# New orders and longer lags in a software-pipelined two-layer attention and expert kernel

## The reference

```python
x = x + L0_xattn(layernorm(x), ctx, ctx)   # 16 heads of 8; q, k, v with biases; softmax; output weights
x = x + L0_ffn(layernorm(x))               # 8 experts, the 2 best by gate; every expert is computed densely
x = x + L1_xattn(layernorm(x), ctx, ctx)   # as the first, without biases
x = x + L1_ffn(layernorm(x))               # recurrent cell over the 128 rows, 64 steps of one tile each
```

## Time and profile before

| | us |
|---|---|
| median of 3 runs | 853.44 |
| lowest, highest | 852.15, 854.73 |
| the profiled execution's own time | 852.91 |
| its span in the profile | 851.1 |
| TensorE busy, mean granted clock | 825.9, 0.994 of full |
| ScalarE busy | 793.9 |
| VectorE busy | 768.9 |
| GpSimd busy | 682.4 |

### The profile page before, as it was taken

One profiled execution on the slowest core, in us unless ns is written; L12 is line 12 of the kernel. 1 busy time (PEld: TensorE's weight loads), 2 busy tenths in 40 slices (PEclk: granted clock), 3 DMA queues, 4 the chain that ended last, 5 costly groups with the idle time before them and its releaser, 6 DMA issues. The chain is left out here.

```text
span 851.1 us, 41480 instructions
## 1 busy us (share of the span) xinstructions
PE 825.9 (97%) x15270; PEld 741.3 (87%) x15270; DVE 768.9 (90%) x2778; ACT 793.9 (93%) x2490; POOL 682.4 (80%) x1292
## 2 busy tenths in 40 slices
PE   6899999999999999999999999999999999999886
PEld 4688899999999999999999999999999999898674
DVE  6789999999999999999999999999999999989845
ACT  5899999999999999999999999999999999989764
POOL 5788988888888888888888888888888888878624
PEclk9999999999999999999999999999999999999999
DMA  9400000000000000000000000000000000000005
GB/s 330 183 3 3 2 3 4 3 3 4 3 3 3 3 4 3 4 3 3 3 3 3 3 3 3 4 3 3 4 3 3 4 3 4 3 3 3 3 3 198
DMA packets 6965, 17.67 MB, mean 21 GB/s; under 512 B 752, under 2 KB 2288, under 8 KB 6768
## 3 DMA queue, kind: packets, MB, share of 16 engines
q1 hardware_dynamic: 6480, 14.44, 4.5%
q10 hardware_dynamic: 288, 0.60, 0.2%
HBM read 10.84 MB, written 4.19 MB: 18 GB/s over the span
## 5 line engine op out<-in xcount | busy, mean ns | idle before, releaser
L824 DVE TENSOR_REDUCE mx<-ps 128x8 f32<-128x512 f32 (+1 forms) x288 | 173.1, 622 | 8.1 <-PE ps L321 7.7
L838 DVE TENSOR_TENSOR Ex<-ps,mx 128x512 f32<-128x512 f32 (+1 forms) x288 | 172.9, 621 | 0.2 <-issue 0.2
L1076 POOL TENSOR_TENSOR h<-Ex 128x512 f32<-128x512 f32 (+1 forms) x144 | 166.9, 1159 | 3.6 <-ACT Ex L632 3.3
L643 ACT ACTIVATE ET<-ps 128x512 f32<-128x512 f32 (+1 forms) x288 | 156.8, 546 | 6.9 <-PE ps L336 6.6
L632 ACT ACTIVATE Ex<-Ex 128x512 f32<-128x512 f32 (+1 forms) x288 | 162.7, 597 | 0.0
L336 PE MATMUL ps<-w,Ex 128*128 128x128 f32 x1024 | 162.3, 277 | 0.0
L681 ACT ACTIVATE hT<-ps,w 128x128 f32<-128x128 f32 x512 | 145.8, 374 | 11.2 <-PE ps L401 4.8
L930 DVE SCALAR_TENSOR_TENSOR acc<-ps,we,acc 128x128 f32<-128x128 f32 x448 | 148.4, 331 | 3.9 <-PE ps L422 1.3
L401 PEld LDWEIGHTS ps<-xT,w 128*128 128x128 f32 x1024 | 124.1, 191 | 24.6 <-issue 24.6
L401 PE MATMUL ps<-xT,w 128*128 128x128 f32 x1024 | 141.8, 281 | 0.0
L1060 POOL TENSOR_TENSOR rs<-ve,half 128x4 f32<-128x4 f32 (+3 forms) x77 | 71.6, 930 | 83.7 <-DVE ve L814 80.6
(11 more groups left out here) (108 smaller groups left out, 1785.7 us busy)
## 6 DMA issues: line engine op xcount, KB each, us to landing
cx<-ctx_dram SPq DMA_DIRECT2D x7, 512.0 KB, 12.9
x<-x_dram SPq DMA_DIRECT2D x7, 512.0 KB, 13.7
out_dram<-x SPq DMA_DIRECT2D x14, 256.0 KB, 2.7
w<-weights_dram SPq DMA_DIRECT2D x2, 512.0 KB, 6.4
w<-weights_dram SPq DMA_DIRECT2D x1, 576.0 KB, 8.7
out_dram<-x SPq DMA_DIRECT2D x4, 128.0 KB, 2.6
w<-weights_dram ACTq DMA_DIRECT2D x1, 328.0 KB, 4.1
w<-weights_dram ACTq DMA_DIRECT2D x1, 256.0 KB, 3.5
```

The costliest lines, as they stand in the source:

```text
L643: e.activation(ET[:, j % 2, r, lo:hi, :, :], b[:, 256 * lo:256 * hi].rearrange("p (c w q) -> p c w q", c=hi - lo, w=2), ACT.Copy).then_inc ...
L824: e.tensor_reduce(mx[:, j % 2, r, 4 * lo:4 * hi], b[:, 256 * lo:256 * hi].rearrange("p (j k) -> p j k", k=64), AX.X, ALU.max).then_inc(sig ...
L838: e.tensor_tensor(Ex[:, j % 2, r, 256 * lo:256 * hi].rearrange("p (j k) -> p j k", k=64), b[:, 256 * lo:256 * hi].rearrange("p (j k) -> p ...
L1076: e.tensor_tensor(u, v[:, :, :, 0:32], v[:, :, :, 32:64], ALU.add).then_inc(sig("half1"), 1)
```

## The change

New orders on all four engines, larger offsets between the parts (6, 10 and 16 instead of 5, 8 and 13) with new lags and bank positions for them, key matmuls behind the new values instead of ahead, the two halves of GpSimd's softmax sums in the other order, the constants' load on ScalarE's queue between weights 0 and 2, the waits for it moved to where the constants are first used, and one matmul on zeros less. What is computed stays the same. The tables `LAG` and `USES` are new throughout; of them only the ends are shown.

```diff
-WARM = 5
+WARM = 4
...
-L1, L2, L3 = 5, 8, 13
-LAG = {"e0": 4, "y1": 3, "sB": 2, "e3": 4, "gate": 1, "turnw": 2, "rt": 4, "e2": 4, "h0": 2, "wx0": 3,
...
+L1, L2, L3 = 6, 10, 16
+LAG = {"sB": 3, "pv": 5, "kv": 2, "h1": 2, "e2": 4, "q": 2, "wx0": 10, "y0": 3, "yb": 3, "e1": 4,
+       "turnx": 1, "e3": 4, "xin": 2, "sA": 2, "e0": 4, "p": 5, "wx1": 7, "turnw": 2, "gate": 1, "y1": 3,
+       "rt": 4, "h0": 2, "S": 2, "ex3": 4, "rT": 5, "ex1": 4, "ex0": 4, "re0": 3, "gB": 3, "sc": 1,
...
-FIRST, LAST = 0, NT + 15
+FIRST, LAST = 0, NT + 19
...
 # sync_program
             load_c(0)
-            load_weights(e, 1)
 # tensor_program, keys_values
-                e.matmul(b[:, 0:128], wkv[:, WK, :], cx[:, t, :], start=True, stop=True)
-                e.matmul(b[:, 256:384], wkv[:, WK1, :], cx[:, t, :], start=True, stop=True, skip_group_check=True)
...
+                e.matmul(b[:, 0:128], wkv[:, WK, :], cx[:, t, :], start=True, stop=True, skip_group_check=True)
+                m = e.matmul(b[:, 256:384], wkv[:, WK1, :], cx[:, t, :], start=True, stop=True, skip_group_check=True)
                 m.then_inc(sig("kv"), 1)
 # turn_x
+                if j == 0:
+                    e.wait_ge(sig("in_w1"), 16)
                 e.wait_ge(sig("n"), j + 1)
 # ahead of the loop
-            e.wait_ge(sig("in_w1"), 16)
 # scalar_program
-            load_weights(e, 0)
-            load_weights(e, 2)
+            for n in (0, 1, 2):
+                load_weights(e, n)
 # gpsimd_program, keys; and not ahead of the loop any more
+                if j == 0:
+                    e.wait_ge(sig("in_w1"), 16)
```

More of the change, by code:

```diff
@@ L505, in tensor_program @@
                     project_bias()
+                step(i, 1)
+                values(i)
+                keys_values(i)
+                hidden(i, 1)
+                turn_e(i, 2)
+                query(i)
+                out_inputs(i, 0)
+                experts(i, 0)
+                expert_bias(i)
+                turn_e(i, 1)
+                turn_x(i)
+                turn_e(i, 3)
+                cell_inputs(i)
+                step(i, 0)
                 turn_e(i, 0)
+                project(i)
+                out_inputs(i, 1)
+                turn_w(i)
+                gate(i)
                 experts(i, 1)
[L508 to L511, removed]
                 turn_r(i)
-                turn_e(i, 2)
                 hidden(i, 0)
-                out_inputs(i, 0)
                 scores(i)
[L517 to L528, removed]
             for n in (5, 6):
@@ L732, in scalar_program @@
                     e.wait_ge(sig("cell"), 1)
+                exps(i, 3)
+                turn_r(i)
                 exps(i, 1)
                 exps(i, 0)
+                relus(i, 0)
+                gates(i, 1)
+                scale(i)
+                keys_values(i)
+                relus(i, 1)
+                turn_e(i, 2)
+                query(i)
                 out_inputs(i, 1)
+                out_inputs(i, 0)
+                turn_e(i, 1)
                 turn_x(i)
+                turn_e(i, 3)
                 widen(i)
+                gates(i, 0)
                 turn_e(i, 0)
-                gates(i, 1)
+                exps(i, 2)
                 turn_w(i)
[L741 to L753, removed]
             e.wait_ge(sig("uo"), 1)
@@ L973, in vector_program @@
                     bias_pieces(2 * (i - FIRST) - 1)
+                gate(i)
+                combine(i, 6)
+                gate_top(i)
+                combine(i, 7)
+                stats_inputs(i)
+                combine(i, 8)
+                gate_index(i)
+                maxima(i, 1)
+                maxima(i, 0)
+                maxima(i, 3)
+                differences(i, 0)
+                differences(i, 1)
+                differences(i, 3)
+                update(i, 1)
+                normal(i)
+                maxima(i, 2)
+                sums(i)
+                differences(i, 2)
+                combine(i, 0)
+                stats_attention(i)
                 combine(i, 1)
[L975 removed]
+                inverse(i)
                 combine(i, 2)
[L977 removed]
+                stats_experts(i)
                 combine(i, 3)
+                spread(i)
                 combine(i, 4)
                 project(i)
+                update(i, 0)
                 combine(i, 5)
[L982 to L1003 removed]
             e.wait_ge(sig("xo0"), SPAN["W0"][1])
@@ L1071, in halves @@
                 e.wait_ge(sig(f"E{2 * g + 1}"), j + 1)
[L1072 to L1073 removed]
+                if 2 * j + 1 - g:
+                    e.wait_ge(sig("half2"), 2 * j + 1 - g)
                 v = Ex[:, s, 2 * g:2 * g + 2, 256 * lo:256 * hi].rearrange("p r (h k) -> p r h k", k=64)
@@ L1141, in gpsimd_program @@
                     e.wait_ge(sig("cleared"), 5)
+                spread(i)
+                halves(i, 1)
+                halves(i, 0)
+                gate_sum(i)
+                add_bias(i)
                 gate_pieces(i)
+                keys(i, 1)
+                keys(i, 0)
                 spread_values(i)
-                add_bias(i)
-                keys(i, 1)
-                halves(i, 0)
-                spread(i)
-                gate_sum(i)
-                halves(i, 1)
-                keys(i, 0)
             e.wait_ge(sig("xo0"), SPAN["W0"][1])
```

37 lines of the change are left out of this document (5 added, 32 removed), and 28 rows, old and new, of tables (LAG, USES).

## The result

| | before | after |
|---|---|---|
| median, us | 852.86 (4 runs) | 870.51 (4 runs) |
| lowest, highest | 852.15, 854.73 | 868.00, 871.28 |
| the profiled execution's own time | 852.91 | 868.00 |
| its span | 851.1 | 866.1 |

The account below looks back on a forecast made before the run. TensorE (PE), busy throughout the 12.21 us middle iterations, was taken as the bound. Edges -10.0, ends +7.5 and start -0.8 sum to -3.3 on 852.91, so 849.6; the forecast was 849.8 us, range 843 to 857.

Parts of the forecast that it names:

- those slacks: Spare time of 0.7 to 1.5 us before bank reuses in the new orders, taken to cover them at no cost.
- 12.04: Length in us forecast for a middle iteration, 0.17 less than the 12.21 before.
- the new edge: Switch from 32x64 tiles (scores) to 128x32 tiles (step 1): one drain of 0.10 and a first round of 0.02.
- The rival of the doubly dear edge: Scores to step 1 costs an exit and an entry, 0.20: iterations of 12.14, 855.7 us in all; chance 0.12.
- The free edge: Rival: scores to step 1 costs nothing, 0.10 less in 59 iterations, middle ones of 11.94, total 844; chance 0.17.
- the term of the edges: Fewer changes between tilings on TensorE save 0.17 in each of 59 iterations: -10.0 us.
- The ends: Longer fill and drain, less three full iterations: net +9.5, less 2 for fewer waits, +7.5 (+3 to +11).
- The start: Constants issued earlier and waited for later put the first turn_x at 6.3: -0.8 us (-0.3 to -1.0).
- ScalarE did not become the bound: Rival: ScalarE sets the iteration, waits at gates 1 make it 12.3, total 862; chance 0.13.
- The slower side: Outcome above 856.0 us; chance 0.18, of which ScalarE 0.13 and part of the double edge 0.05.
- 857 as an upper end: Top of the forecast range, taking in most of the double-edge case and leaving out ScalarE's 862.

Follow-up runs that it names:

- a_pin_away: Changed kernel with 18 already-met waits added to TensorE's queue in every iteration, to keep instruction fetches away from the scores: 869.41 us, ratio 1.0179.
- a_apart2: Changed kernel with the hidden layer's first half between scores and step 1, the banks kept as they were: 912.96 us, ratio 1.0697.
- b_dense: Kernel before with every matmul of the values' product made twice: 920.40 us, ratio 1.0785.
- a_gate: Changed kernel with the second expert half ahead of gate and turn_w instead of behind them: 859.15 us, ratio 1.0071.
- b_long: Kernel before with only the offsets 6, 10 and 16 instead of 5, 8 and 13, old orders and lags: 861.63 us, ratio 1.0096.
- b_start: Kernel before with only the changed start (constants on ScalarE's queue, their waits moved, one matmul on zeros less): 854.59 us, ratio 1.0016.
- a_pin_hit: Changed kernel with 18 added waits, left out in the first three iterations and partly in the fourth, to fetch instructions inside the scores: 890.31 us, ratio 1.0435.
- a_pin_on: Changed kernel with 18 added waits an iteration, left out in the first two; fetches mostly started ahead of the scores: 871.45 us, ratio 1.0214.
- a_apart: Changed kernel with the hidden layer's first half between scores and step 1, bank positions moved with it: 1028.07 us, ratio 1.2064.

## Why the prediction was wrong

**The step that failed** is the sentence in which I costed the new orders themselves at nothing, with "the cover is those slacks". I laid out who waits for whom and found 0.7 us or more everywhere. Those slacks held: in a_pin_away, with the new order, no matmul waits in 200 us of the middle, and in the kernel after only for "issue". But the order also fixes which instructions stand next to each other, and that had two prices.
- **The breaks, 9.1 us.** 17 to 64 is 580.2 after and 571.1 in a_pin_away. The same instructions have 0 or 33 breaks by where the packet starts, and every stop ends 1.2 to 1.7 us after the packet's record. A long run of small tiles makes it worse: the kernel before has no break with 104 matmuls in a row, a_apart2 with 104 has three small ones, the change with 136 nine, b_dense with 168 sixteen. "New values, step 0, values' product" was already dense, and I read it for edges alone, not for how many instructions it takes in a microsecond. That TensorE runs out of instructions is the reading that fits all of these; the fill level of its buffer is in no record, so the size that decides stays open.
- **The small matmuls, 0.11 an iteration, 5.2 us over the middle.** bf16 turn_w and the 8-column gate stand ahead of the experts. a_gate took it back by putting them behind.

**The edges were nearly right, and 12.04 in part by luck.** Scores to step 1 is 1.05 (406.95 to 408.00), as forecast with one drain for the new edge, and step 0 alone is 0.47. But step 1 to values' product is 0.43 where 0.37 was named, 0.09 more than between two of its kind: with the 0.10 in the scores the new edge costs 0.19, where 0.12 was forecast and the rival had 0.20 and a first round more. With the small matmuls back behind the experts the iteration is 12.03 against 12.04 forecast: 0.18 saved, not 0.17. Of these, 0.05 have nothing to do with an edge. The bf16 bias matmul stood ahead of the first experts and now stands behind them, which the prediction did not count; they take 0.95 (421.16 to 422.11) before and 0.90 (412.22 to 413.12) after:

```profile
421.10 0.22 PE L434 MATMUL ps<-b2s,weT 72*128 72x128 bf16 x1
421.16 1.11 PE L422 MATMUL ps<-w,hT 128*128 128x128 f32 x8
...
412.22 1.06 PE L423 MATMUL ps<-w,hT 128*128 128x128 f32 x8
413.12 0.22 PE L435 MATMUL ps<-b2s,weT 72*128 72x128 bf16 x1
```

So the edges together saved about 0.13 to 0.14. The rival of the doubly dear edge named just the 12.14 that the plain iteration shows, but not for its reason: a_gate takes 0.11 of it away without touching that edge. One number of an iteration is met by more than one cause, and the distances at the edge itself tell them apart. The free edge fell. The rule of the Trainium skill, "TensorEngine Tiling (Array Packing)", Tiling Modes, Key Properties, that a change of tiling mode drains the engine, agrees with the 1.05 and the 0.43 here.

But the term of the edges was too large by 2.0: I applied 0.17 to 59 iterations, 12 of them outside the 47 of the middle, and after's fill and drain equal b_long's within 0.4 us, so no saving shows there.

**The ends were mis-sized by up to 2.3.** The rows gave +9.5, I took 2 off for fewer waits. b_long gives +9.8 by the profiled executions and +8.0 by the medians, so the term missed by 0.5 to 2.3, and whether the correction was wrong stays open between these two.

**The start was right in place, not in worth.** The first turn_x is at 5.96 (6.3 forecast), -1.2 instead of -0.8. But b_start shows that such a gain need not arrive at the end.

**ScalarE did not become the bound.** It had 0.13 as the way to slower. At 12.03 no matmul waits for it.

The sum on the profiled executions: 868.0 less the 849.6 of the prediction is 18.4. The middle is 580.2 against 47 x 12.04 = 565.9, 14.3 (9.1 and 5.2); the partial iterations 2.0; the ends 2.3; the start 0.2 to 0.4 the other way: 18.3. The profiled execution is the fastest of the four, and the 2.5 us from it to the median 870.51 are not in this sum. The slower side had a chance, but not with this mechanism, and 857 as an upper end took in no case in which the order itself costs something.

## What to carry to other kernels

When small matmuls are drawn together to save changes of tiling, count the instructions of the longest run and its length in microseconds, beside the edges: a saving of 0.18 per iteration was given back by breaks of 0.5 to 1.2 us in one iteration of five. Read "issue" gaps against the instruction packets of the engine's queue; if the gaps follow them, a few spare instructions in a loop can move the fetch to a place where it does no harm, and the trace has to show where it landed. And cut a reordered kernel into fill, middle and drain against a kernel with the offsets alone, so that each term of the sum has its own measurement, and look at the granted clock of the fill before its time is put down to the code.

## What the runs showed that I had not expected

- TensorE's instructions arrive in packets of 16 KB on a queue of their own (125 in the kernel after, each 0.9 to 1.5 us), all through the run, and PE can stop behind one with nothing else in its way: 33 times in the middle of a_pin_hit, with start-to-start distances of 0.45 to 1.29 us. PE goes on 1.2 to 1.7 us after the packet's record has ended. A packet that started 0.5 us or more ahead of the dense run did no harm (a_pin_on).
- Instructions that do nothing (waits already met) are free in a middle iteration bound by matmuls (18 of them: 12.15 without and with). In the ends of a_pin_away, which had them everywhere, 7.4 and 4.2 us more were spent, the first of them with 23.9 us at the lower clock against 3.4, so only the second is a sign that they cost something there.
- Two records of the 8-column gate and one of bf16 ahead of eight float32 matmuls cost 0.13 more than behind them (1.45 and 1.32 for the four groups); the one bf16 record of the bias ahead of eight costs 0.05 more (0.95 and 0.90).
- Moving one bank use cost 20% (a_apart), by a wait of 1.8 us per iteration on an engine that the moved work has nothing to do with, and with it stretches at the lower clock in 30 of 47 iterations.
